# Second cross attention: the padding mask as three bf16 rows instead of one fp32 row

## What is computed

```python
qh = (q @ Wq + bq).reshape(b, -1, H, HD)          # H = 16 heads, HD = 16, q: 2 x 1024 tokens
kh = (k @ Wk + bk).reshape(b, -1, H, HD)          # 64 context tokens
vh = (v @ Wv + bv).reshape(b, -1, H, HD)
qk = einsum('bjhd,bkhd->bhjk', qh, kh) / sqrt(HD)
qk = qk + padding_mask * -1000000000000.0         # padding_mask: (2, 1, 1, 64)
out = einsum('bhjk,bkhd->bjhd', softmax(qk, -1), vh) @ Wo + bo
```

## Time and profile before

| | |
|---|---|
| time, median of 3 runs | 3511.59 us (3508.27 to 3514.3) |
| profiled execution, its own time | 3526.84 us |
| its span in the trace | 3524.6 us |
| PE / DVE / ACT / POOL busy, share of the span | 81% / 59% / 41% / 39% |
| mean granted TensorE clock over the span | 0.905 |

### The profile page before, as it was taken

How to read it: one execution, slowest core, us unless ns; L and a number is a source line. 1 busy time by engine, 2 the same in 40 slices (tenths; PEclk the granted TensorE clock), 3 DMA queues, 4 the chain that set the end, 5 groups by cost and what they waited for, 6 DMA issues and landing times. The chain is left out here.

```text
span 3524.6 us, 30222 instructions
## 1 busy us (share of the span) xinstructions
PE 2867.8 (81%) x8560; PEld 1248.7 (35%) x8560; DVE 2089.9 (59%) x2977; ACT 1436.8 (41%) x2168; POOL 1370.2 (39%) x1138
## 2 busy tenths in 40 slices
PE   5888988888775877999999829999478887779966
PEld 1232332333222543222222228888132332226522
DVE  1899999999995436444444230000339999932233
ACT  4566556655643322333333302221246555422233
POOL 2588788778774012000000140000437788720010
PEclk8999999999998978999999959999589999986688
DMA  1222022012200002100100224444221022000000
GB/s 62 94 96 93 26 96 102 32 71 96 79 18 18 1 14 90 28 19 20 26 18 19 69 97 142 179 180 142 79 96 63 35 96 96 0 18 0 0 7 24
DMA packets 67914, 215.28 MB, mean 61 GB/s; under 512 B 15517, under 2 KB 40361, under 8 KB 48697
## 3 DMA queue, kind: packets, MB, share of 16 engines
q1 hardware_dynamic: 61384, 181.12, 14.4%
q10 hardware_dynamic: 3312, 24.12, 2.0%
q0 software_dynamic: 3072, 8.39, 0.7%
HBM read 187.97 MB, written 25.43 MB: 61 GB/s over the span
## 5 line engine op out<-in xcount | busy, mean ns | idle before, releaser
L750 POOL TENSOR_TENSOR s_dbu<-s_dx,s_bc 128x512 f32<-128x512 f32 x768 | 975.0, 1275 | 313.3 <-DVE s_psum L490 312.3
L420 PE MATMUL s_psum<-s_hc,ident 128*128 128x512 f32 x1536 | 850.2, 638 | 209.9 <-DVE s_hc L506 209.1
L639 ACT ACTIVATE s_psum<-s_dt,s_a_neg 128x512 f32<-128x512 f32 x768 | 526.5, 690 | 631.0 <-DVE s_hc L506 630.2
L506 DVE TENSOR_TENSOR s_hc<-s_psum,s_bc 128x512 f32<-128x512 f32 x768 | 519.5, 677 | 0.9 <-issue 0.6
L420 PEld LDWEIGHTS s_psum<-s_hc,ident 128*128 128x128 f32 x1536 | 240.0, 190 | 764.4 <-DVE s_hc L506 686.0
L490 DVE TENSOR_TENSOR_SCAN s_psum<-s_psum,s_state,s_dbu 128x512 f32<-128x512 f32 x384 | 490.5, 1277 | 10.2 <-ACT s_psum L639 10.2
L490 DVE TENSOR_TENSOR_SCAN s_psum<-s_psum,s_dbu 128x512 f32<-128x512 f32 x384 | 468.5, 1220 | 12.8 <-ACT s_psum L639 9.9
L1329 DVE TENSOR_REDUCE s_umax<-s_banks 128x1 f32<-128x512 f32 (+3 forms) x384 | 210.3, 554 | 282.6 <-PE s_banks L1195 223.5
L1233 PE MATMUL s_banks<-s_probs,s_vs 128*17 128x512 f32 (+3 forms) x768 | 324.4, 512 | 35.6 <-ACT s_ot L1410 32.3
L1419 ACT ACTIVATE s_probs<-s_banks 128x512 f32<-128x512 f32 (+3 forms) x384 | 187.3, 489 | 395.7 <-PE s_banks L1219 295.5
L1780 ACT ACTIVATE s_hidden<-s_banks,s_w 128x256 f32<-128x256 f32 x184 | 77.1, 470 | 302.8 <-PE s_banks L1603 302.8
(11 more groups left out here) (249 smaller groups left out, 3626.0 us busy)
## 6 DMA issues: line engine op xcount, KB each, us to landing
s_bc<-fwd_rows SPq DMA_DIRECT2D x64, 1024.0 KB, 4.8
s_bc<-m_rows SPq DMA_DIRECT2D x32, 1024.0 KB, 4.7
s_w<-in_moe_w SPq DMA_DIRECT2D x23, 1028.0 KB, 7.3
s_w<-in_moe_w ACTq DMA_DIRECT2D x23, 1024.0 KB, 5.6
s_stack<-qk_parts SPq DMA_DIRECT2D x192, 64.0 KB, 2.1
qk_parts<-s_parts SPq DMA_DIRECT2D x48, 128.0 KB, 1.8
moe_in_rows<-s_zero SPq DMA_DIRECT2D x1, 5888.0 KB, 19.1
s_xs<-moe_in_rows SPq DMA_DIRECT2D x23, 256.0 KB, 6.0
```

The costliest lines, as they stand in the source:

```text
L420: pe.matmul(psum[:, SCANS + block_no % 2, :], consts["ident"][:], hc[:, unit % PRODUCTS, :], start=(n == 0), stop=(n == NS - 1)).then_inc( ...
L506: dve.tensor_tensor(hc[:, unit % PRODUCTS, :], psum[:, unit % SCANS, :], bc[:, 2 * n + 1, :], ALU.mult)\
L639: act.activation(psum[:, unit % SCANS, :], dt[:, g % 2, i // NS, :], ACT.Exp, scale=a_neg[CHUNKS[g][0]][:, i:i + 1]).then_inc(decay_ready, 1)
L750: pool.tensor_tensor(dbu[:, unit % TERMS, :], dx[:, g % 2, i // NS, :], bc[:, 2 * n, :], ALU.mult)\
```

## The change

In the call with `causal` false, the mask is multiplied by -4e12 once, on DVE, and split into three bf16 rows whose sum is the fp32 value (value, rest, rest of the rest). Since the three parts are made on partition 0, SP moves them to the three partitions of `maskb` with three small DMAs. PE waits for these ahead of the main loop. The mask matmul of line 886 then is bf16, three rows of ones times `maskb`, one MATMUL instead of two. The causal call gets the new tiles and semaphores, and its `memset` is of `ones3` in place of `neg4`; nothing else changes there.

```diff
--- before.py
+++ after.py
@@ -810,7 +810,10 @@
         keys = s.sb("keys", [P, KD, B * SK])
         kd = s.sb("kd", [P, B, KD, HB, SK])
         vd = s.sb("vd", [P, B, PAIRS, 2 * HD + 2])
-        neg4 = s.sb("neg4", [1, P])
+        mask_f = s.sb("mask_f", [1, 2, B * SK])
+        mask_parts = s.sb("mask_parts", [1, 3, B * SK], BF16)
+        maskb = s.sb("maskb", [3, B, SK], BF16)
+        ones3 = s.sb("ones3", [3, P], BF16)
         ones_row = s.sb("ones_row", [1, P])
         qs = s.sb("qs", [P, 2, KD, P])
         nmax = s.sb("nmax", [P, 2, H])
@@ -825,7 +828,7 @@
         turned_o = s.psum("turned_o", [P, CH])
         banks = scores[:].rearrange("p u c t -> p (u c) t")
 
-        made = s.sem("made")
+        made, mask_step, mask_stored = s.sem("made"), s.sem("mask_step"), s.sem("mask_stored")
         q_ready, q_free = s.sem("q_ready"), s.sem("q_free")
         k_ready, k_stored, kd_ready = s.sem("k_ready"), s.sem("k_stored"), s.sem("kd_ready")
         v_ready, vd_ready = s.sem("v_ready"), s.sem("vd_ready")
@@ -837,6 +840,13 @@
         block = s.block()
         NT = B * QT
         N_LOAD = (5 + 2 * B) * 16
+
+        @block.sync
+        def _(sp):
+            if not causal:
+                sp.wait_ge(mask_step, 5)
+                for part in range(3):
+                    sp.dma_start(maskb[part:part + 1, :, :], mask_parts[:, part, :]).then_inc(mask_stored, 16)
 
         @block.tensor
         def _(pe):
@@ -869,6 +879,8 @@
             pe.wait_ge(kd_ready, B * KD)
             pe.wait_ge(made, 3)
             pe.wait_ge(vd_ready, B)
+            if not causal:
+                pe.wait_ge(mask_stored, 3 * 16)
             with pe.Fori(0, B) as b:
 
                 def score(i):
@@ -883,8 +895,8 @@
                                            late[:, i, :].unsqueeze(1).to_broadcast([P, HB, SK]),
                                            start=False, stop=True)
                         else:
-                            mm = pe.matmul(scores[:, u, hb, :], neg4[:],
-                                           key_mask[:, b, :].unsqueeze(1).to_broadcast([1, HB, SK]),
+                            mm = pe.matmul(scores[:, u, hb, :], ones3[:],
+                                           maskb[:, b, :].unsqueeze(1).to_broadcast([3, HB, SK]),
                                            start=False, stop=True)
                     mm.then_inc(scored, 1)
 
@@ -937,10 +949,22 @@
         def _(dve):
             for sem in (moved, on_ready):
                 dve.sem_inc(sem, 1)
-            dve.memset(neg4[:], -4e12).then_inc(made, 1)
+            dve.memset(ones3[:], 1.0).then_inc(made, 1)
             dve.memset(ones_row[:], 1.0).then_inc(made, 1)
             dve.wait_ge(loaded, N_LOAD)
             dve.tensor_copy(late[:], late_f).then_inc(made, 1)
+            if not causal:
+                full, rest = mask_f[:, 0, :], mask_f[:, 1, :]
+                dve.tensor_scalar(full, key_mask[:].rearrange("o b s -> o (b s)"), -4e12, None, ALU.mult)\
+                   .then_inc(mask_step, 1)
+                dve.wait_ge(mask_step, 1)
+                dve.tensor_copy(mask_parts[:, 0, :], full).then_inc(mask_step, 1)
+                dve.wait_ge(mask_step, 2)
+                dve.tensor_tensor(rest, full, mask_parts[:, 0, :], ALU.subtract).then_inc(mask_step, 1)
+                dve.wait_ge(mask_step, 3)
+                dve.tensor_copy(mask_parts[:, 1, :], rest).then_inc(mask_step, 1)
+                dve.wait_ge(mask_step, 4)
+                dve.tensor_tensor(mask_parts[:, 2, :], rest, mask_parts[:, 1, :], ALU.subtract).then_inc(mask_step, 1)
             dve.sem_inc(out_free, 4)
             dve.wait_ge(k_stored, KD)
             for b in range(B):
```

## The result

The changed kernel takes 3452.01 us (median of 4 runs, 3447.17 to 3462.93) against 3510.43 us before (4 runs, one more than in the table ahead of the prediction): ratio 0.9837, 95% interval 0.9809 to 0.9864. That is 58 us less; the forecast was 3466 us, within 3446 to 3488. The profiled execution took 3456.23 us, its span 3454.0 us at a mean clock of 0.921.

A forecast was written before the change was run, and what follows sets the result against it. PE was taken to bound the second cross attention loop, falling from 175.9 to 130 us. From the median 3511.6, minus 46 for the loop, plus 0.2 for semaphore clears, gives 3466 us, range 3446 to 3488.

The forecast's parts named there:

- the first rival: Second cross attention loop: switches cost nothing, score pair back to 0.86 us, loop 112.9, saved 63, total 3449 us; chance 0.14.
- The prices of the passes: Second loop on PE: mask pass 0.32 us at full clock, 0.60 at half; score pairs 1.06 and 2.00; tile 6.46.
- What a switch costs: Second loop on PE: each switch between 128 rows and one costs about 0.10 us, the weight load standing open.
- The setup: Start of the block: five DVE operations of 0.9 to 1.8 us, three DMAs and PE's new wait, costed at nothing.
- The cover: Start of the block: DVE's 2.07 us wait for the keys covers the five new operations of 0.9 to 1.8 us.
- f: Second loop: share of time at full clock, 0.32 before, 0.78 in the first loop, taken as 0.55 after the change.
- the formula: Loop time of 16 tiles: 16 / (f/full + (1-f)/half), with full and half the tile times at each clock; forecast 126 us.
- the ends of the batches: Second loop: draining at the ends of the two batches, 4 us added to the formula's 126 us.
- The reason given for the clock: Second loop: one-row passes fill PE but don't hold the clock up; taking half their instructions away lifts f.
- The second rival: Second loop: clock share doesn't move, f stays 0.32; loop 142 us, saved 34, total 3478 us; chance 0.3.
- The third: Rival, second loop: clock stays at 0.50 throughout, loop 181 us, or 194 with total 3530 us; slower by the clock, chance 0.03.
- The half-way value: Second loop: full-clock share f taken as 0.55, the middle between 0.32 and 0.78.

## Why the prediction was right, and where it was off

**The time came out right, the loop didn't.** The forecast was a loop of 121 to 139 us at a mean clock of 0.72 to 0.85; measured were 114.5 and 0.93, and the total of 3452 us lies closer to the first rival's 3449 than to the forecast of 3466. It is inside the range because the range was drawn down to 3446 to take in that rival, whose reason (switches that cost nothing) is out. That much of it is luck.

**The prices of the passes** held: the mask pass 0.32 us at full clock as forecast, 0.54 at half against an estimate of 0.60; score pairs 1.05 and 2.00 as before; full-clock tile 6.41 against 6.46. What a switch costs was read too low: it was put at 0.10, but a pair and its mask pair together lie (1.06 + 1.05) - 2 x 0.86 = 0.39 over the price without switches, for two switches, and in the changed kernel (1.05 + 0.32) - (0.86 + 0.21) = 0.30. So it is 0.15 to 0.20 each. The sum didn't suffer, because it took the 0.32 from the earlier trace rows and the 1.06 as it stood. The first rival, switches that cost nothing, fell with these rows, though the loop's length came out near its 112.9 us. The Trainium skill's statement that a matmul of 32 rows takes the time of one of 128 (TensorE: Matmul & The Clock Gate, "Why this matters for your kernels") holds for the stream itself, not for the pass in its place: a second three-row pass behind the first adds 0.53 - 0.32 = 0.21, as much as a pass of 128 rows, but a single one between score pairs costs 0.32, the difference being the switches on both sides.

**The setup** costed at nothing was nothing: shown alone, it leaves the loop at 175.9 us. The cover that I named is the right one, and 0.85 us of it is left.

**The term that was mis-sized is f,** the share of time at the full clock, for which I took the middle, 0.55, between the two loops. It was 0.86 (mean clock 0.93). With the measured tile the formula gives 16 / (0.86/6.41 + 0.14/10.81) = 109 us, and the measured 114.5 leaves 6 us for the ends of the batches, where I took 4. At f = 0.32 it would have been 142. So about 34 of the 61 us come from the shorter pass at the old clock, and about 27 from the clock; I had counted 34 and 12. This is why the time came out 14 us under the forecast. The split depends on the order: with the old pass at the new share the formula gives 16 / (0.86/7.85 + 0.14/13.61) = 134 us and some 6 for the ends, so 36 us for the clock and 25 for the pass.

The formula also spreads the half clock evenly over the tiles, and the traces don't. In the changed kernel 13.6 of the 15.5 us at half lie at the change of batch and the rest at the end. In the first loop of the kernel before, from which f = 0.78 was taken, it is 10.2 us at the change of batch, 8.3 at the end and only 6.8 inside the second batch. So the two loops that were averaged differed less in a share than in whether the clock is lost inside a batch at all.

**The reason given for the clock** was right in kind: the one-row passes fill PE, but don't hold the clock up. With 64 rows at the same prices the clock is 0.86, with one row 0.66. Why rows should count is not shown by any run. The second rival, a clock share that doesn't move because L895 and the transposes set it, is out by that pair and by the run with full fp32 rows. The third, a clock that never comes up without the dense fp32 pair, is out as well: with less of it the clock came up. The Trainium skill's rule in Part 1 of the same page, that a busy engine keeps the full clock, disagrees with this kernel beyond the rows of before: PE was busy for 169.6 of 175.9 us at 0.66, and for 100.2 of 114.5 us at 0.93. The kernel with less busy time has the higher clock.

**The half-way value was too cautious** because I took the three-row pass to hold the clock down nearly as the pair had done. At 0.32 us a half it doesn't: the loop is near the level of the first cross attention (0.91 and 0.89), which has 128 rows there. Doubled to 0.53 us, it brought the clock to 0.75 in the one execution with a trace, the slowest of four, and this is no state in between: the first batch ran at 1.00 and the second at 0.61. What the passes seem to decide is whether the full clock survives inside a batch and how soon it is back behind the drain. I had no row for that.

## What to carry to other kernels

A matmul of few rows can cost more than its columns: between full-row matmuls its weight load and the one behind it were not hidden (64 rows and fewer here), and enough of such time in a loop cost the full clock. Where PE is dense and yet granted less than the full clock, look for such passes first, and shorten them (bf16 parts), fill their rows, or fold them into an operand made once ahead of the loop. Before costing a saved pass at its duration alone, compare the mean clock of the loop with that of a sister loop without it.

## What the runs showed of the hardware

- Rows alone move the clock: the same fp32 passes at the same prices gave a mean clock of 0.66 with one row and 0.86 with 64; 96 and 128 rows, without the switches, 0.88 each.
- 96 rows beside 128 cost no switch (loop 133.4 us with both). An fp32 pair beside passes of one, three or 64 rows cost 1.05 us instead of 0.86, and a three-row bf16 pass 0.32 instead of 0.21.
- With a doubled three-row pass, 12 us of dense scores at half clock didn't bring the full clock back in one execution; with the pass taken once, one score did, in two.
- The same instructions ran at the full clock in one batch (51.1 us at 1.00) and mostly at half in the next (47.8 us at 0.50, PE busy for 45.96 of them), in the execution with the doubled pass.
- Some loops were reproduced within 0.1 us in separate executions (175.9 twice, 114.5 and 114.6), but the first loop, the same in all traces, took 109.7 to 114.5 us. The start of the second loop, behind code that is the same but for the setup of the mask, moved between 3137.8 and 3162.0 us. Part of the gap of 70.6 us between the two profiled executions is of that kind.
